# Contracting attention 1's q, k and v over 128 features and twice 64, in 5 passes where there were 6

## What is computed

```python
h = tok(x)                                   # 64 x 197 x 192
y = _layernorm(h)                            # rows of 192 features
qkv = y @ w_qkv.T                            # 192 -> 3 * 768
q, k, v = split(qkv)                         # 12 heads of 64 each
q = q * rsqrt(norm(q, axis=heads) + EPS);  k likewise
out = softmax(q k^T / scale) v
h = h + out @ w_out.T + b_out
h = h + moe_attention(_layernorm(h))
```

## Time and profile before

| | us |
|---|---|
| median of 3 runs | 4334.95 (4316.67 to 4337.84) |
| the profiled execution's own time | 4333.73 |
| its span, first to last instruction | 4331.8 |
| PE busy | 3840.3 (89%) |
| PEld busy | 3175.7 (73%) |
| DVE busy | 2706.7 (62%) |
| ACT busy | 2232.1 (52%) |
| POOL busy | 524.0 (12%) |

### The profile page before, as it was taken

One profiled execution on the slowest core, in us unless ns is written; L12 is line 12 of the kernel. 1 busy time (PEld: TensorE's weight loads), 2 busy tenths in 40 slices (PEclk: granted clock), 3 DMA queues, 4 the chain that ended last, 5 costly groups with the idle time before them and its releaser, 6 DMA issues.

```text
span 4331.8 us, 98533 instructions
## 1 busy us (share of the span) xinstructions
PE 3840.3 (89%) x38552; PEld 3175.7 (73%) x38552; DVE 2706.7 (62%) x6866; ACT 2232.1 (52%) x3969; POOL 524.0 (12%) x858
## 2 busy tenths in 40 slices
PE   4999998889988998989999889899888898899888
PEld 3777777777777777777777777777777777777776
DVE  4666666566566666665665666666656656656654
ACT  1555555555555555545545555555555555555553
POOL 1110111111101101101111011011111111111110
PEclk7999999999999999999999999999999999999997
DMA  2000000000000000000000000000000000000000
GB/s 76 8 16 8 16 8 15 15 10 14 15 8 15 16 8 15 15 8 15 8 15 16 8 15 15 8 16 15 9 15 10 14 15 10 14 15 8 15 4 4
DMA packets 26198, 60.41 MB, mean 14 GB/s; under 512 B 3534, under 2 KB 16465, under 8 KB 25714
## 3 DMA queue, kind: packets, MB, share of 16 engines
q1 hardware_dynamic: 25806, 54.14, 4.1%
HBM read 44.45 MB, written 9.68 MB: 12 GB/s over the span
## 4 chain that ended last, share of the span: by engine, by line
PE 72%; DVE 17%; issue 4%; ACT 4%; POOL 1%; DMA 0%; SPq 0%; DVEq 0%; ACTq 0%; POOLq 0%
PE psum L584 13%; DVE mx L922 9%; PE psum L590 7%; PE psum L513 6%; PE psum L523 6%; PE psum L618 6%; PE psum L496 6%; PE psum L557 5%; PE psum L541 3%; PE psum L648 3%; PE psum L641 2%; PE psum L620 2%; PE psum L621 2%; ACT ka L769 2%; PE psum L571 2%
## 5 line engine op out<-in xcount | busy, mean ns | idle before, releaser
L922 DVE TENSOR_REDUCE mx<-psum 99x4 f32<-99x788 f32 x768 | 707.2, 972 | 67.3 <-PE psum L541 40.3
L732 ACT ACTIVATE ebuf<-psum 99x788 f32<-99x788 f32 x768 | 605.8, 825 | 175.7 <-PE psum L573 163.9
L513 PE MATMUL psum<-hn_s,qk_w 96*128 96x197 f16 x4608 | 435.8, 252 | 1.2 <-DVE hn_s L888 1.2
L440 POOL TENSOR_TENSOR veps<-mv,eps_ln 99x2 f32<-99x2 f32 x256 | 49.9, 195 | 3169.2 <-DVE mv L831 2552.9
L696 ACT ACTIVATE qk_sq<-psum 128x788 f32<-128x788 f32 x192 | 159.1, 828 | 516.0 <-PE psum L513 516.0
L513 PEld LDWEIGHTS psum<-hn_s,qk_w 96*128 96x128 f16 x4608 | 406.2, 99 | 8.8 <-DVE hn_s L888 1.5
L618 PE MATMUL psum<-hn_s,qkv_w 96*128 96x197 f16 x2304 | 342.2, 254 | 44.2 <-ACT ss L705 43.1
L523 PE MATMUL psum<-v_w,hn_s 96*99 96x384 f16 x1536 | 333.6, 376 | 30.3 <-DVE mx L922 21.8
L943 DVE TENSOR_TENSOR qk<-psum,rinv 128x197 f32<-128x197 f32 x384 | 137.9, 359 | 342.1 <-ACT rinv L741 342.1
L590 PE MATMUL psum<-out_w,qk 128*99 128x192 f32 x1536 | 286.8, 348 | 61.5 <-issue 61.3
L584 PE MATMUL psum<-ebuf,vx 98*64 98x197 f32 (+1 forms) x3072 | 332.6, 336 | 0.0
(11 more groups left out here) (164 smaller groups left out, 8006.3 us busy)
## 6 DMA issues: line engine op xcount, KB each, us to landing
xb<-x_t SPq DMA_DIRECT2D x64, 591.0 KB, 3.8
out<-h SPq DMA_DIRECT2D x128, 73.5 KB
vx<-w_qk SPq DMA_DIRECT2D x1, 1152.0 KB
out<-h SPq DMA_DIRECT2D x64, 0.8 KB
qk<-w_qkv SPq DMA_DIRECT2D x1, 720.0 KB
qk_sq<-w_emb SPq DMA_DIRECT2D x1, 576.0 KB
v_raw<-w_v SPq DMA_DIRECT2D x1, 576.0 KB
out_w<-w_out SPq DMA_DIRECT2D x1, 576.0 KB
```

Of the source, the lines that this page charges most:

```text
L513: mm = nc.tensor.matmul(ps(p, slice(0, 128), slice(at, at + NT), m // 2), qk_w[:, w, c, f:f + 128], hn_s[s][:, v, c, 0:NT], start=(n == 0) ...
L732: nc.scalar.activation(ebuf[n % EBUFS][:].rearrange("p e a t -> p e (a t)"), psum[0:TR, b:b + 2, 0:2 * NT], ACT.Exp).then_inc(done, 1)
L922: nc.vector.tensor_reduce(mx[s][:, :, 2 * i:2 * i + 2].rearrange("p a e -> p e a"), psum[0:TR, b:b + 2, 0:2 * NT].rearrange("p e (a t) -> ...
```

## The change

q, k and v are contracted over a chunk of 128 features and a chunk of 64. The 64 rows of the small chunk stand twice in the moving or stationary operand that comes from `hn` (rows 64 to 127 repeat rows 0 to 63), and the weights' third plane holds the high half in rows 0 to 63 and the low half in rows 64 to 127. One matmul over 128 rows so gives high and low weights at once, and the sum has 3 matmuls for the large chunk and 2 for the small one (high and low half of `hn`).

- `hn` becomes 256 columns wide. A new ACT instruction in step LC copies columns 128 to 191 to 192 to 255 and signals `hn_doubled`.
- T1 transposes two chunks of 128 columns; ahead of the second it waits for `hn_doubled`. ACT's and DVE's reads of T1 have 128 partitions for 96.
- QK has 4 by 5 matmuls of 128 rows for 4 by 6 of 96; V has 2 by 5 for 2 by 6. T2 and attention 2 stay at two chunks of 96.
- The constants: w_qk and w_v are loaded in 4 DMAs each, the last 64 rows twice; both groups now stand last in the list of loads. DVE splits the large chunk as before and builds the third plane with one scaling and one subtraction on rows 64 to 127.

```diff
-        qk_w = sb("qk_w", [HC, 2, 2, 2 * INNER], F16)
-        v_w = sb("v_w", [HC, 2, 2, INNER], F16)
+        qk_w = sb("qk_w", [128, 3, 2 * INNER], F16)
+        v_w = sb("v_w", [128, 3, INNER], F16)
...
+        hn_both = two("hn", [TR, 2, 256])
+        hn = [hn_both[s][:, :, 0:D] for s in range(2)]
+        hn_s = two("hn_s", [128, 2, 2, NTP], F16)
...
+        for raw, w in ((qk_raw, w_qk), (v_raw, w_v)):
+            loads += [(raw[0:HC, 0:1, :], w[:, 0:1, :]), (raw[HC:128, 0:1, :], w[0:128 - HC, 1:2, :]),
+                      (raw[0:64, 1:2, :], w[128 - HC:HC, 1:2, :]), (raw[64:128, 1:2, :], w[128 - HC:HC, 1:2, :])]
...
+            PACKED = ((0, 0, 0), (0, 1, 0), (1, 0, 0), (2, 0, 1), (2, 1, 1))
...
                     elif kind == "T1":
                         wait(pe, now, hn_ready, ("LC", s, 0))
-                        mm = hidden_transposed(p, hn[s])
+                        for c in range(2):
+                            if c == 1:
+                                wait(pe, now, hn_doubled, ("LC", s, 0))
+                            for t in range(2):
+                                n = key_rows(t)
+                                at = NT * c + TO * t
+                                src = hn_both[s][0:n, t, 128 * c:128 * c + 128]
+                                mm = nc.tensor.transpose(ps(p, slice(0, 128), slice(at, at + n)), src,
+                                                         ident[0:n, 0:n])
                     elif kind == "QK":
...
-                            for n, (c, w, v) in enumerate((c, *wv) for c in range(2) for wv in SPLIT):
+                            for n, (w, v, c) in enumerate(PACKED):
                                 mm = nc.tensor.matmul(ps(p, slice(0, 128), slice(at, at + NT), m // 2),
-                                                      qk_w[:, w, c, f:f + 128], hn_s[s][:, v, c, 0:NT],
-                                                      start=(n == 0), stop=(n == 5))
+                                                      qk_w[:, w, f:f + 128], hn_s[s][:, v, c, 0:NT],
+                                                      start=(n == 0), stop=(n == 4))
...
                     elif kind == "V":
                         for b in range(2):
-                            for n, (c, w, v) in enumerate((c, *wv) for c in range(2) for wv in SPLIT):
+                            for n, (w, v, c) in enumerate(PACKED):
...
+                    elif kind == "LC":
+
+                        wait(act, now, hn_ready, p)
+                        nc.scalar.copy(hn_both[s][:, :, D:256], hn_both[s][:, :, 128:D]).then_inc(hn_doubled[1], 1)
...
+            for w, raw in ((qk_w, qk_raw), (v_w, v_raw)):
+                split_weights(lambda v: w[:, v], raw[:, 0])
+                nc.vector.tensor_scalar(w[:, 2], raw[:, 1], WS, None, ALU.mult).then_inc(setup_w, 1)
+                splits[0] += 1
+                dve.wait_ge(setup_w, splits[0])
+                nc.vector.scalar_tensor_tensor(out=w[64:128, 2], in0=raw[64:128, 1], scalar=WS, in1=w[64:128, 2],
+                                               op0=ALU.mult, op1=ALU.subtract)
```

More of the change, by code:

```diff
@@ L179, in vit_tower @@
         h0, h1 = two("h0", [TR, 2, D]), two("h1", [TR, 2, D])
-        hn = two("hn", [TR, 2, D])
-        hn_s, hn2_s = two("hn_s", [HC, 2, 2, NTP], F16), two("hn2_s", [HC, 2, 2, NTP], F16)
+        hn_both = two("hn", [TR, 2, 256])
+        hn = [hn_both[s][:, :, 0:D] for s in range(2)]
+        hn_s = two("hn_s", [128, 2, 2, NTP], F16)
+        hn2_s = two("hn2_s", [HC, 2, 2, NTP], F16)
         qk = two("qk", [128, H, NT])
@@ L200, in vit_tower @@
         hn2_t = [ss[s][0:HC] for s in range(2)]
-        vx_both = sb("vx", [TR, 2, 2, H, DH])
-        vx = [vx_both[:, s] for s in range(2)]
+        vx_both = sb("vx", [128, 2, 2, H, DH])
+        vx = [vx_both[0:TR, s] for s in range(2)]
         ones_col = sb("ones_col", [TR, DH])
@@ L521, in body @@
                         for b in range(2):
-                            for n, (c, w, v) in enumerate((c, *wv) for c in range(2) for wv in SPLIT):
+                            for n, (w, v, c) in enumerate(PACKED):
                                 mm = nc.tensor.matmul(ps(p, slice(0, TR), slice(0, INNER // 2), b),
                                                       hn_s[s][:, v, c, tile_cols(i)],
-                                                      v_w[:, w, c, INNER // 2 * b:INNER // 2 * (b + 1)],
-                                                      start=(n == 0), stop=(n == 5))
+                                                      v_w[:, w, INNER // 2 * b:INNER // 2 * (b + 1)],
+                                                      start=(n == 0), stop=(n == 4))
                     elif kind == "SM":
@@ L683, in body @@
                         wait(act, now, pe_sig[kind], p)
-                        src = psum[0:HC, b, 0:2 * NT].rearrange("p (c t) -> p c t", c=2)
+                        rows = slice(0, 128 if kind == "T1" else HC)
+                        src = psum[rows, b, 0:2 * NT].rearrange("p (c t) -> p c t", c=2)
                         dst = hn_s if kind == "T1" else hn2_s
@@ L813, in _ @@
             nc.vector.tensor_scalar(bias2_raw[:, 0], bias2_raw[:, 0], WS, None, ALU.mult).then_inc(setup_w, 1)
-            dve.wait_ge(setup_w, 5)
+            dve.wait_ge(setup_w, splits[0] + 1)
             nc.vector.tensor_copy(bias2_w[:], bias2_raw[:, 0]).then_inc(setup_w, 1)
-            dve.wait_ge(setup_w, 6)
+            dve.wait_ge(setup_w, splits[0] + 2)
             nc.vector.scalar_tensor_tensor(out=bias2_w[:], in0=bias2_w[:], scalar=low_row, in1=bias2_raw[:, 0],
@@ L888, in body @@
                         nc.vector.tensor_tensor(dst[:, 1, :, 0:NT],
-                                                psum[0:HC, b, 0:2 * NT].rearrange("p (c t) -> p c t", c=2),
-                                                dst[:, 0, :, 0:NT], ALU.subtract).then_inc(done, 1)
+                                                psum[0:128 if kind == "T1" else HC, b, 0:2 * NT].rearrange(
+                                                    "p (c t) -> p c t", c=2), dst[:, 0, :, 0:NT], ALU.subtract).then_inc(done, 1)
                     elif kind == "S":
```

11 lines of the change are left out of this document (5 added, 6 removed).

## The result

The changed kernel takes 4272.15 us (median of 4 runs; before 4336.4 in the runs beside them), the ratio is 0.9856 [0.9818, 0.9894]. One of the four (4487.23 us, at a granted clock of 0.846) is left out of the ratio, and so is one of 13188.78 us in the last experiment. Timed again in other rounds the changed kernel took 4263.5 us, ratio 0.9866 [0.9847, 0.9885]: 1.3 to 1.4% faster. The profiled execution took 4271.2 us, span 4269.3 (before: 4331.8), mean granted clock 0.962.

What follows compares the result with a forecast made beforehand. PE bounds most of a half, with chained waits and falls of the clock. From 4333.7 us, savings of 52.3 and 3 more for set-up give 4284; 13 less for fewer OP falls gives 4271 us, range 4238 to 4335.

Steps and rivals of the forecast that it cites:

- QK.0 and QK.2 at nothing, QK.1 at 0.28 us: Four passes fewer per QK group: QK.0 and QK.2 save nothing, hidden beside DVE's work; QK.1 saves 0.28 us a half.
- V at the high clock or with the short fall: Score stage: V.1 saves 0.33 us at the high clock, V.0 0.25 where the clock comes back within it.
- V with the long fall, 1.76: Score stage, clock staying low past V.0: 1.76 us saved if it returns at V.0's end, lower bound 1.01.
- T1, 0.11: T1's four transposes, on PE's path, take 128 columns for 96: 0.11 us a half more, bounds 0 and 0.2.
- The copy: ACT's copy ahead of T1: hidden with 0.7 us to spare; rival, T1 0.3 us late a half, 4290, chance 0.03.
- Set-up, 3: Loading and splitting the constants before the loop: 3 us more, bounds 0 and 8.
- The number of falls: Clock falls at OP behind the loop's end gap: half of 16 go, 8 x 1.6 = 13 us saved.
- The slow rival: Clock falls in PE's wait ahead of T2: 4337 for half the halves, 4390 for all 64; chances 0.12 and 0.08.
- (a): Behind OP's product, ahead of T2: PE idles 1.46 us for DVE's normalised rows, forecast to grow to 1.80.

Runs made afterwards that it cites:

- the last experiment: Changed kernel with six passes of 128 rows in both QK and V, the last one done twice: 4311.2 us, 0.9954 of the kernel before.
- one wait: Changed kernel with PE waiting ahead of T1 for the doubled copy alone, ACT's copy kept: 4265.3 us, 0.9858 of the kernel before.
- filler: Changed kernel with eight more passes of 384 columns on PE ahead of the scores SM2.0, computing nothing: 4301.2 us, 0.9937 of the kernel before.
- both: Changed kernel with eight filling passes ahead of SM2.0 and PE waiting only for the doubled copy ahead of T1: 4310.0 us, 0.9958 of the kernel before.

## Why the prediction was right

It said 4271, and 62.3 us off the profiled execution; that came to 62.5 (58 in the timing again, by the medians). Where the time is won was right: at QK.1, at V and in the falls, not at QK.0 and QK.2. That the number was met to less than 1 us is luck: some of its terms are wrong and cancel.

- *QK.0 and QK.2 at nothing, QK.1 at 0.28 us.* Right in kind. QK.1 gives 0.23 at G and 0.18 at PS, below the bounds of 0.25 to 0.34: the saving shrinks on the way, G itself taking 1.14 us for 1.09. 64 x 0.1 = 6 us too much.
- *V at the high clock or with the short fall.* Right: odd halves, which had the short fall before and after, went from 63.66 to 63.19; less QK.1's 0.18 that is 0.29 for 0.25 to 0.33.
- *V with the long fall, 1.76.* Right, and with the reason given (V.0's rows): with the fall at the same place it is long in 51 of 52 at 96 rows and in none of 35 in the changed kernel. Twelve passes of 128 rows leave one long fall, ten of 96 bring them back in 19 halves.
- *T1, 0.11.* Wrong: nothing. 7 us too much on the costs.
- *The copy.* It doesn't hold T1 up, but with it (or PE's wait for it) the gap at each loop's end is still 0.3 us longer, 9 us. Not in the prediction.
- *Set-up, 3.* Too small, and covered by something that I hadn't counted. DVE starts at 31.14 us for 27.25, and the first image's embedding, q and k start 4.6 to 4.7 us later. Those q and k then take 6.84 us for 9.39 (60 passes for 72, partly at the low clock), and by the loop's start 1.4 us is left.
- *The number of falls.* Right in sum, wrong in kind. I kept the 15 good iterations and shortened the 16 bad ones. In fact the short fall came to nearly all even halves (26 of 32, none before), 0.8 us each (66.34 for 65.54, the latter two halves only), also where there had been none: 12 halves without a fall before the end became 4, 6 us lost. Why the clock now falls at V.0 in nearly every half isn't shown. Nor did the long fall and the OP fall come together in all 16 halves before the change, as I had said, but in 15. For that OP's falls went from 15 to 4, where I took half of them away: 5 us more won. Added up, these corrections come to 8 us less gain where the total was met, so each is good to a few microseconds only.
- *The slow rival* (the clock falls in (a)) had 20 in 100. It stayed away for the reason I had put against it, that QK's passes fill 128 rows, and the run with 96 shows it. The rule of the Trainium skill that spoke for it ("TensorE: Matmul & The Clock Gate", Part 4: PE-mode transpose) was not what decided: T2's transposes stand behind the gap in all kernels, and with 128 rows around them the clock stayed up in 60 of 63 halves, with 96 in 5. Whether they count for less than other matmuls, no run here shows.

How the 1.34% of the timing again divide can be estimated from the last run: what the rows, T1 and the set-up bring with as many passes as before is 0.46% [0.24, 0.69], 20 us; the passes saved on top of that bring the other 0.88%, 38 us (about 0.6 to 1.2% by both intervals). The 20 are themselves a balance: the loop's end took 13.5 back (74.8 us of idle time for 61.3), so the falls that went gave some 33, worked out from the halves and not measured apart.

## What to carry to other kernels

Where an engine's clock depends on its work, ask of a saved instruction not only whether it lies on the path, but what idle time it opens and what stands on either side: the same five passes made the kernel 1.3% faster with full rows and 1.1% slower with three quarters of them in QK. Moving work from a place where it seems to cost something into a free gap can open an idle time that costs more: V.0 in the gap was to save at most 33 us of waits and cost 118. And count stalls by kind over all repetitions before and after: one removed often returns at the next gap.

## What the hardware showed that I had not expected

- The rows of a matmul count for the clock: ten passes of 384 columns leave it low behind them in 19 of 63 halves with 96 rows, in none of the changed kernel's with 128 (in 2 without the copy); QK's 96 rows for 128 give 58 falls for 4 at most in any run with 128, behind the same idle time of 1.8 us.
- The clock falls in a stretch of 1.6 us of idle time, 1.2 us of work and 0.7 us of idle time or right behind it (57 of 63 halves of the changed kernel), and nearly never behind one of 1.83 us with full rows around it (3 of 63). Length of the gap alone doesn't tell.
- The gap of PE at the loop's end, for which the view of waits names no releaser, changes with the code around it, from 2.08 us (no copy) over 2.42 and 2.50 (changed, twice), 2.58 (one wait) and 2.95 (filler) to 3.34 (both) as means of 29. At each stands a 16 KB instruction transfer of 1.0 to 1.2 us, and OP starts 1.7 to 1.8 us behind its landing; with two transfers the gap is 3.3 to 4.2 us long. Why the second one comes stays open.
- A transpose of 98 rows takes 251 ns with 128 columns held and 252 with 96.
